# Five steps of a two-block transformer kernel put elsewhere in their engines' order, and one small transfer issued first

## The chip, the core and the metric

The kernel runs on one core of a Trainium2 chip. A core has a matrix engine (PE, TensorE), a vector engine (DVE, VectorE), an activation engine (ACT, ScalarE), a general engine (POOL, GpSimd) and a queue engine that only issues transfers (SP, SyncE). Each engine works through its own list of instructions in the order in which they are written; between engines there are only semaphores. The metric is the device time in microseconds (us), and less is better.

## The reference, cut to what matters

`x` is (16 sequences, 128 tokens, 128 channels) in float32, and `cond` is (16, 128). Two blocks follow each other.

```python
# block 0: one head of 128 channels, RMS norm, exact gelu
h = film(rmsnorm(x, norm1_w), cond, film1_w, film1_b)      # scale and shift for each sequence
x = x + (softmax(Q @ K.T * D**-0.5) @ V) @ proj_w + proj_b
h = film(rmsnorm(x, norm2_w), cond, film2_w, film2_b)
x = x + gelu(h @ mlp_w1 + mlp_b1) @ mlp_w2 + mlp_b2
# block 1: 16 heads of 8 channels, layer norm, padding mask, gates
mod = silu(cond) @ ada_w.T + ada_b                          # six rows for each sequence
h = modulate(layernorm(x), shift_msa, scale_msa)
x = x + gate_msa * attention(h, padding_mask)
h = modulate(layernorm(x), shift_mlp, scale_mlp)
x = x + gate_mlp * (gelu_tanh(h @ fc1_w.T + fc1_b) @ fc2_w.T + fc2_b)
```

## The kernel before

The whole of `x` stays in SBUF as `xs` (tokens on the partitions, 16 sequences). Tokens of one sequence are a tile of 128x128, and four sequences are a group, so that there are four groups `g` of `G = 4`. The order of the work is written out by hand, engine by engine; nothing schedules it. There are four stages, and the letter in front of a semaphore's name tells the stage.

Stage a is the attention of block 0, by groups. For a group, DVE takes statistics of `xs` (`statistics`, L844 to L854), POOL raises them to a power (`root`, L1115) and normalises (`norm`, L1134, into `xn`), PE turns the four tiles (`a_norm`, L239), ACT applies the film scale and shift (`affine`, L661, into `hT`), PE multiplies for Q and K (`a_qk`, L265) and for V (`a_value`, L270). DVE copies Q out of PSUM (`a_q`, L907), ACT copies K and V out (`a_kv`, L668 and L670). PE makes the scores (`a_scores`, L278), DVE their maxima (`a_max`, L913), ACT the exponentials (`a_exp`, L676), PE turns these (`a_turn`) and weights the values with them (`a_weighted`, L291), and DVE adds the result into `xs` (`a_residual`, L928). On PE the next group's products are interleaved: scores of group g, then Q, K and V of group g + 1, then turning and weighting of g. For group 0 alone, half of the normalising and of the film step is on DVE (L887, L892). After the first group's residual DVE also computes `silu` of the condition (L950, L952, L954), which PE needs only for the `ada` products behind the last group (L536).

Stage b is the MLP of block 0: `m_norm` (L239), `b_up` (four products of 128x512, L307, one for each quarter f of the hidden width), `b_gelus` on ACT (L703), `b_down` (L315), `b_residual` on DVE (L963).

Stage c is the attention of block 1, by sequences b = 0 to 15. Queries and keys are spread by transfers into padded tensors `q_pad`, `k_pad`, so that a head is 8 rows of a strip of 32. In a step b, PE does `first_slot(b)` (32 small products: half the scores of b and half the transposed scores of b - 2, L366), `between(b)` (four small steps of earlier or later sequences: `back_a`, `turn_maxima`, `back_b`, `turn_x` or `back_c`), `second_slot(b)` (the other halves), and `behind(b)` (`weighted(b - 3)`, L432, and one product of the next group's Q, K or V: `project`, L353, L356, L360). DVE takes the maxima (L1002), which each slot waits for because it writes the same PSUM banks again. ACT takes exponentials (L739), copies, and the modulation of a coming sequence (`front_h`, L718). POOL normalises coming sequences (`front_x`, L1189), prepares `x + gate * bias` (`prepare`, L1194, L1196) and adds the gated attention (`residual`, L1200, L1203). DVE takes the statistics of a finished sequence (`next_statistics`, L1019).

Stage d is the MLP of block 1. Its first normalisation, `d_norm(0)` and `d_norm(1)` (four instructions of L867 each), stands on DVE behind the steps 11 and 14 of stage c. PE turns the result in `m_norm("d_", 0, 6)`, behind step 12, and in `m_norm("d_", 1, 5)`, behind `weighted(B - 3, 4)` at the end of stage c. `d_bias` on POOL (L1214, L1217) prepares the last residual.

ACT's queue begins with three transfers: the film weights with the condition (L649), the bias rows (L650), the mask rows as integers (L651, 16 partitions of 128 numbers).

## Time and profile before

| what | value |
|---|---|
| median of 3 runs | 193.1 us (192.03 to 194.94) |
| the profiled execution's own time | 191.69 us |
| its span in the profile | 189.9 us |
| busy in that span | PE 173.1 us (91%), DVE 121.1 (64%), ACT 107.7 (57%), POOL 98.7 (52%) |
| stage a ends, about | 38.8 us |
| stage b's last up-product ends, about | 64 us |
| steps 2 to 15 of stage c | 77.2 to 148 us |

The span is what the profile covers, from the first instruction to the last; 1.8 us of the execution's time lie outside it. Busy shares are averages over four stages that differ, so the table tells which engine works most, and not where it waits.

### The profile page before, as it was taken

What the parts mean: (1) busy time and instruction counts of PE and PEld (TensorE: products, weight loads), DVE (VectorE), ACT (ScalarE), POOL (GpSimd) and SP (SyncE); (2) the same over time, 40 slices, a digit from 0 to 9 for tenths busy, and PEclk for the clock granted to TensorE, in tenths of its full rate; (3) what the DMA queues carried; (4) which work ended last, traced back from release to release, by engine and by line L of the source; (5) the groups of instructions that cost most, each with busy time, mean ns of one, the idle gap of its engine ahead of it and who ended that gap; (6) DMA issues with size and microseconds to landing.
All of it is one profiled execution on the core that took longest, in us unless ns stands there. A gap on an engine that the chain in (4) does not pass through costs nothing.

```text
span 189.9 us, 5687 instructions
## 1 busy us (share of the span) xinstructions
PE 173.1 (91%) x2250; PEld 134.2 (71%) x2250; DVE 121.1 (64%) x357; ACT 107.7 (57%) x272; POOL 98.7 (52%) x166
## 2 busy tenths in 40 slices
PE   6876989999699999889999999996997999999993
PEld 6744877587276698677678777875886765678592
DVE  0693598978005069768756876699489665596233
ACT  2336957862683751577577756673774785723500
POOL 5599949899900805994004333675145086691000
PEclk9999999999999999999999999998899999999999
DMA  5999999412650300300110000100000000001103
GB/s 126 345 430 423 433 412 431 177 43 52 217 224 0 114 0 3 116 5 5 57 60 3 7 35 31 57 5 2 5 7 7 2 3 0 5 0 55 59 0 110
DMA packets 5190, 19.31 MB, mean 102 GB/s; under 512 B 556, under 2 KB 1148, under 8 KB 3836
## 3 DMA queue, kind: packets, MB, share of 16 engines
q1 hardware_dynamic: 4844, 18.27, 25.0%
q10 hardware_dynamic: 320, 0.68, 1.2%
q8 instruction: 18, 0.29, 0.7%
q14 instruction: 8, 0.07, 0.1%
HBM read 7.24 MB, written 1.09 MB: 44 GB/s over the span
## 4 chain that ended last, share of the span: by engine, by line
PE 44%; issue 20%; POOL 19%; DVE 9%; DMA 3%; ACT 3%; POOLq 0%; DVEq 0%; ACTq 0%
PE ps L337 8%; PE ps L328 7%; PE ps L315 6%; PE ps L307 6%; POOL xb L1196 3%; POOL gtmp L1194 3%; POOL xc L1189 3%; PE ps L265 3%; POOL rstd L1115 3%; PE ps L366 2%; DMA xs<-x 2%; POOL xs L1203 2%; POOL gated L1200 2%; ACT hT L661 2%; DVE bn L844 2%
## 5 line engine op out<-in xcount | busy, mean ns | idle before, releaser
L1002 DVE TENSOR_REDUCE nm<-ps 128x4 f32<-128x512 f32 x64 | 42.0, 683 | 18.3 <-PE ps L366 17.9
L739 ACT ACTIVATE shared<-ps 128x512 f32<-128x512 f32 x64 | 34.5, 596 | 22.0 <-PE ps L366 21.9
L366 PE MATMUL ps<-k_pad,q_pad 32*128 32x128 f32 x512 | 35.4, 284 | 5.0 <-DVE nm L1002 4.7
L366 PEld LDWEIGHTS ps<-k_pad,q_pad 32*128 32x128 f32 x512 | 30.1, 188 | 13.2 <-issue 6.5
L366 PE MATMUL ps<-q_pad,k_pad 32*128 32x128 f32 x512 | 35.5, 285 | 0.1
L366 PEld LDWEIGHTS ps<-q_pad,k_pad 32*128 32x128 f32 x512 | 29.7, 188 | 0.5 <-DMA q_pad<-nmT 0.5
L1115 POOL TENSOR_TENSOR rstd<-var_eps,half 128x4 f32<-128x4 f32 x16 | 16.4, 1023 | 24.5 <-DVE var_eps L858 17.0
L1200 POOL TENSOR_TENSOR gated<-attn,gate 128x128 f32<-128x128 f32 x16 | 7.3, 459 | 40.8 <-ACT attn L758 40.7
L432 PE MATMUL ps<-shared,vx 128*32 128x128 f32 x512 | 17.9, 282 | 0.5 <-ACT attn L758 0.3
L785 ACT ACTIVATE hid<-ps,W 128x512 f32<-128x512 f32 x16 | 10.9, 689 | 9.7 <-PE ps L328 9.7
L307 PE MATMUL ps<-hT,W 128*128 128x512 f32 x32 | 14.6, 598 | 1.7 <-ACT hT L661 1.7
L661 ACT ACTIVATE hT<-ps,shift,scale 128x128 f32<-128x128 f32 x34 | 12.9, 467 | 5.2 <-PE ps L239 4.1
L432 PEld LDWEIGHTS ps<-shared,vx 128*32 128x32 f32 x512 | 13.6, 112 | 3.2 <-issue 1.7
L337 PEld LDWEIGHTS ps<-W,hid 128*128 128x128 f32 x128 | 14.7, 192 | 1.0 <-issue 1.0
L328 PE MATMUL ps<-hT,W 128*128 128x512 f32 x32 | 15.3, 599 | 0.0
L315 PE MATMUL ps<-W,hid 128*128 128x128 f32 x128 | 15.2, 276 | 0.0
L315 PEld LDWEIGHTS ps<-W,hid 128*128 128x128 f32 x128 | 14.8, 192 | 0.6 <-issue 0.5
L703 ACT ACTIVATE hid<-ps,W 128x512 f32<-128x512 f32 x16 | 10.7, 688 | 7.9 <-PE ps L307 7.8
L337 PE MATMUL ps<-W,hid 128*128 128x128 f32 x128 | 14.8, 275 | 0.0
L1189 POOL TENSOR_SCALAR xc<-xs,mean,rstd 128x128 f32<-128x128 f32 x16 | 12.6, 797 | 0.4
L844 DVE BATCH_NORM_STATS2 bn<-xs 128x6 f32<-128x128 f32 x44 | 9.5, 277 | 4.4 <-DMA xs<-x 4.2
L867 DVE TENSOR_SCALAR xn<-xs,stat,rstd 128x128 f32<-128x128 f32 x16 | 11.0, 749 | 1.7 <-POOL rstd L1115 1.7
(127 smaller groups left out, 321.9 us busy)
## 6 DMA issues: line engine op xcount, KB each, us to landing
q_pad<-hid SPq DMA_DIRECT2D x1, 4096.0 KB, 21.7
k_pad<-hid SPq DMA_DIRECT2D x1, 4096.0 KB, 30.6
gate<-gates SPq DMA_DIRECT2D x1, 2048.0 KB, 7.2
xs<-x SPq DMA_DIRECT2D x4, 256.0 KB, 6.4
gate<-mask SPq DMA_DIRECT2D x1, 1024.0 KB, 11.9
q_pad<-apT SPq DMA_DIRECT2D x4, 256.0 KB, 2.4
k_pad<-apT SPq DMA_DIRECT2D x4, 256.0 KB, 2.4
W<-weights SPq DMA_DIRECT2D x1, 768.0 KB, 9.9
```

What stands on the lines that cost most here:

```text
L307: mm(ps[:, f, :], w("mlp1", C, C * f), hT[g % 2][:], start=True, stop=True).then_inc(s["b_M1"], 1)
L315: ins = mm(bank(5)[:, j], hid[g % 2][:, f, j], w("mlp2", C, C * f), start=(f == 0), stop=(f == FC - 1), skip_group_check=True)
L328: mm(ps[:, UP_BANK[n], :], w("fc1", C, C * f), hT[g % 2][:], start=True, stop=True)\
L337: ins = mm(bank(o_bank)[:, j], hid[g % 2][:, f, j], w("fc2", C, C * f), start=(f == 0), stop=(f == FC - 1), skip_group_check=True)
L366: return mm(bank(to)[:, t], held[some, t, b], moved[some, t, b], start=True, stop=True, skip_group_check=True)
L432: ins = mm(ps[32 * j:32 * j + 32, to, N * e:N * e + N], v[:, e, j, s2], p[:, e, j, s2], start=(s2 == 0), stop=(s2 == 1), skip_group_check= ...
L661: ins = a(hT[g % 2][:, j], src[:, j], ACT.Identity, bias=shift[:, k, b:b + 1], scale=scale[:, k, b:b + 1])
L739: a(pT[b % 2][:, r], bank(of), ACT.Exp, scale=HD ** -0.5).then_inc(s["c_exp"], 1)
L844: v.bn_stats(bn[:, j], xs[:, G * g + j]).then_inc(ok, 1)
L1002: v.tensor_reduce(nm[b % 2][:, 4 * r:4 * r + 4], bank(of), AX.X, ALU.max, negate=True).then_inc(s["c_max"], 1)
L1115: p.tensor_tensor(rstd[:, k, G * g:G * g + G], var_eps[:, k, G * g:G * g + G], half[:, 0:G], ALU.pow)\
L1189: p.tensor_scalar(xc[b % 4][:], xs[:, b], mean[:, 0, b:b + 1], rstd[:, 2, b:b + 1], ALU.subtract, ALU.mult)\
```

## The change

Six edits, and no arithmetic is added or removed.

1. ACT's queue issues the mask rows first, the film weights second and the bias rows third.
2. In stage a, ACT copies K and V of group 0 ahead of the film step of group 1.
3. DVE computes `silu` ahead of its wait for the first turned tiles, and no longer behind the first residual.
4. In stage b, group 1: two of the four up-products, then the turning of group 2, then the other two; on ACT two gelus, the film step of group 2, two gelus.
5. The V product of the second group in stage c (four matmuls and their copy to `vx`, in bank 6) is cut in two halves of two matmuls, in bank 7, in the middle of the steps 2 and 3; the wait for it in `between(3)` goes, and `behind(b)` waits for it from b = 3 on.
6. `d_norm(0)` and `d_norm(1)` leave DVE; POOL does them as `first_norm` behind its `residual` of the steps 11 and 15, and `d_bias(0)` moves from step 11 to step 12.

```diff
--- before.py
+++ after.py
@@ -148,7 +148,7 @@
             ada_mm ada_ok gate_ok  wvp_mm wvp_ok bias_ok bcol_ok pbias_ok zero_ok pad_zero aug_ok aug_out aug_in maskb_ok c_vinit
             a_pow a_xn a_xb a_T a_h a_Q a_K a_V a_qT a_kT a_v a_S a_max a_exp a_PT a_pT a_PV a_rden a_res
             b_pow b_xn b_xb b_T b_h b_M1 b_gelu b_M2 b_res
-            c_pow c_xb c_gp c_xc c_Tx c_h c_Q c_K c_V c_q c_k c_v c_qs c_ks
+            c_pow c_xb c_gp c_xc c_Tx c_h c_Q c_K c_V c_q c_k c_v c_qs c_ks c_vh
             c_S c_max c_NT c_nm c_nms0 c_nms1 c_T c_exp c_PV c_oT c_T2 c_rden c_on c_T3 c_onT c_pr c_at c_ga c_res c_st
             d_var d_pow d_xn d_xb d_T d_h d_M1 d_gelu d_M2 d_gm d_gp d_res""".split()
         s = {n: sem(n) for n in names}
@@ -298,8 +298,8 @@
                     pe.wait_ge(s[p + "h"], g)
                 transposes(bank(t_bank), xn[g % 2], s[p + "T"])
 
-            def b_up(g):
-                for f in range(FC):
+            def b_up(g, fs=range(FC)):
+                for f in fs:
                     if f == 0:
                         pe.wait_ge(s["b_h"], g + 1)
                     if g:
@@ -361,6 +361,13 @@
                              skip_group_check=True)
                 ins.then_inc(s["c_V"], 1)
 
+            def second_value(half):
+                if half:
+                    pe.wait_ge(s["c_vh"], 1)
+                for j in (2 * half, 2 * half + 1):
+                    mm(ps[:, 7, N * (j % 2):N * (j % 2) + N], hc[1][:, j], w("v1"), start=True, stop=True,
+                       skip_group_check=True)
+
             def heads(held, moved, b, r, t, to):
                 some = slice(TILE * r, TILE * r + TILE)
                 return mm(bank(to)[:, t], held[some, t, b], moved[some, t, b], start=True, stop=True, skip_group_check=True)
@@ -454,7 +461,7 @@
             def between(b):
 
                 g = b - 1
-                if g % G < 3 and g // G + 1 < B // G:
+                if g % G < 3 and g != 2 and g // G + 1 < B // G:
                     pe.wait_ge(s[("c_q", "c_k", "c_v")[g % G]], g // G + 2)
                 if b == 13:
                     pe.wait_ge(s["d_h"], 1)
@@ -465,6 +472,8 @@
                     back_b(b - 5)
                 if b + LEAD < B:
                     pe.wait_ge(s["c_h"], b + LEAD)
+                    if b in (2, 3):
+                        second_value(b - 2)
                     turn_x(b + LEAD)
                 if b >= 6:
                     back_c(b - 6)
@@ -472,7 +481,7 @@
             def behind(b):
 
                 if b >= 3:
-                    pe.wait_ge(s["c_v"], (b - 3) // G + 1)
+                    pe.wait_ge(s["c_v"], max(2, (b - 3) // G + 1))
                     pe.wait_ge(s["c_h"], min(b + LEAD + 1, B))
                     if b >= 5:
                         pe.wait_ge(s["c_onT"], b - 4)
@@ -484,7 +493,7 @@
 
             def project(b):
                 g = b // G + 1
-                if g < B // G and b % G < 3:
+                if g < B // G and b % G < 3 and b != 2:
                     if b:
                         pe.wait_ge(s["c_nm"], b)
                     if b >= 4:
@@ -544,8 +553,9 @@
             mm(ps[:, 7, 3 * C:4 * C], bcol1[:], w("proj1"), start=False, stop=True, skip_group_check=True)\
                 .then_inc(s["ada_mm"], 1)
             b_down(0)
-            b_up(1)
+            b_up(1, range(2))
             m_norm("b_", 2, 4)
+            b_up(1, range(2, FC))
             b_up(2)
             m_norm("b_", 3, 4)
             pe.wait_ge(s["a_res"], B)
@@ -646,9 +656,9 @@
         @block.scalar
         def _(act):
             a = nc.scalar.activation
+            act.dma_start(mask_ri[:], mask).then_inc(s["mask_rin"], 16)
             act.dma_start(W[:, 0:W_AT["q"]], weights[:, 0:W_AT["q"]]).then_inc(s["w_film"], 16)
             act.dma_start(R[:, :], rows.partition_broadcast(128)).then_inc(s["rows_in"], 16)
-            act.dma_start(mask_ri[:], mask).then_inc(s["mask_rin"], 16)
 
             act.wait_ge(s["w_film"], 16)
             a(cond_e[:], w("cond", B), ACT.Exp, scale=-1.0).then_inc(s["silu_e"], 1)
@@ -683,8 +693,8 @@
             affine("a_", 0, 0, bank(0), range(2))
             act.wait_ge(s["wvp_mm"], 1)
             a(wvp[:], ps[:, 6, 0:C], ACT.Copy).then_inc(s["wvp_ok"], 1)
+            a_kv(0)
             affine("a_", 1, 0, bank(0))
-            a_kv(0)
             a_exp(0)
             for g in range(1, 4):
                 a_kv(g)
@@ -695,8 +705,8 @@
                 a_exp(g)
 
 
-            def b_gelus(g):
-                for f in range(FC):
+            def b_gelus(g, fs=range(FC)):
+                for f in fs:
                     act.wait_ge(s["b_M1"], FC * g + f + 1)
                     if g > 1:
                         act.wait_ge(s["b_M2"], g - 1)
@@ -705,8 +715,9 @@
             b_gelus(0)
             affine("b_", 1, 1, bank(4))
             act.wait_ge(s["pad_zero"], 32)
-            b_gelus(1)
+            b_gelus(1, range(2))
             affine("b_", 2, 1, bank(4))
+            b_gelus(1, range(2, FC))
             b_gelus(2)
             affine("b_", 3, 1, bank(4))
 
@@ -724,9 +735,16 @@
                     act.wait_ge(s["c_ks"], 16 * g)
                 a(k_sb[:], bank(K_BANK[g]), ACT.Identity, bias=col("cols1", COL1["k_b"])).then_inc(s["c_k"], 1)
 
+            def second_v(half):
+                v = ps[:, 7, 0:2 * N].rearrange("n (a k d) -> n a k d", k=2, d=HD)
+                slots = vx[1][:].rearrange("n b (a z) -> n (b a) z", z=64)[:, 16 * half:16 * half + 16]
+                for k in range(2):
+                    ins = a(slots[:, :, 48 * k:48 * k + HD], v[:, :, k], ACT.Copy)
+                ins.then_inc(s["c_v" if half else "c_vh"], 1)
+
             def front_v(g):
 
-                act.wait_ge(s["c_V"], g + 1)
+                act.wait_ge(s["c_V"], g + 1 if g < 2 else g)
                 v = ps[:, V_BANK[g], :].rearrange("n (a k d) -> n a k d", k=2, d=HD)
                 slots = vx[g % 2][:].rearrange("n b (a z) -> n (b a) z", z=64)
                 for k in range(2):
@@ -765,6 +783,8 @@
                     turned_o(b - 5)
                 if 0 < b and b + LEAD < B:
                     front_h(b + LEAD)
+                if b in (2, 3):
+                    second_v(b - 2)
                 if b >= 6:
                     projected(b - 6)
                 if b >= 2:
@@ -774,7 +794,7 @@
                     back_o(b - 3)
                 if b % G == 1 and b // G + 1 < B // G:
                     front_k(b // G + 1)
-                elif b % G == 2 and b // G + 1 < B // G:
+                elif b % G == 2 and b > 2 and b // G + 1 < B // G:
                     front_v(b // G + 1)
 
             def d_gelu(g, f):
@@ -886,6 +906,12 @@
             for j in range(2, G):
                 ins = v.tensor_scalar(xn[0][:, j], xs[:, j], rstd[:, 0, j:j + 1], None, ALU.mult)
             ins.then_inc(s["a_xd"], 1)
+            dve.wait_ge(s["silu_e"], 1)
+            v.tensor_scalar(cond_s[:], cond_e[:], 1.0, None, ALU.add).then_inc(s["silu_one"], 1)
+            dve.wait_ge(s["silu_one"], 1)
+            v.reciprocal(cond_r[:], cond_s[:]).then_inc(s["silu_one"], 1)
+            dve.wait_ge(s["silu_one"], 2)
+            v.tensor_tensor(silu[:], w("cond", B), cond_r[:], ALU.mult).then_inc(s["silu_ok"], 1)
             dve.wait_ge(s["a_T"], 1)
             dve.wait_ge(s["film_ok"], 2)
             for j in range(2, G):
@@ -944,14 +970,6 @@
                     a_max(g + 1)
                 a_residual(g)
                 dve.wait_ge(s["a_res"], G * (g + 1))
-                if g == 0:
-
-                    dve.wait_ge(s["silu_e"], 1)
-                    v.tensor_scalar(cond_s[:], cond_e[:], 1.0, None, ALU.add).then_inc(s["silu_one"], 1)
-                    dve.wait_ge(s["silu_one"], 1)
-                    v.reciprocal(cond_r[:], cond_s[:]).then_inc(s["silu_one"], 1)
-                    dve.wait_ge(s["silu_one"], 2)
-                    v.tensor_tensor(silu[:], w("cond", B), cond_r[:], ALU.mult).then_inc(s["silu_ok"], 1)
 
             statistics(1, 3)
 
@@ -1060,8 +1078,6 @@
             statistics(2, 3)
             for b in range(2, B):
                 step(b)
-                if b in (11, 14):
-                    d_norm((b - 11) // 3)
             turned_max(B - 1)
             normalise(B - 4)
             sums(B - 3)
@@ -1217,6 +1233,13 @@
                 p.tensor_tensor(xb[:, b:b + G], xs[:, b:b + G], gtmp[:], ALU.add).then_inc(s["d_xb"], 1)
                 pool.wait_ge(s["d_xb"], g + 1)
 
+            def first_norm(g):
+                pool.wait_ge(s["d_pow"], g + 1)
+                for j in range(G):
+                    b = G * g + j
+                    ins = p.tensor_scalar(xn[g][:, j], xs[:, b], stat[:, b, 0:1], rstd[:, 3, b:b + 1], ALU.subtract, ALU.mult)
+                ins.then_inc(s["d_xn"], 1)
+
             for b in range(B):
                 if b + LEAD + 1 < B:
                     if (b + LEAD + 1) % G == 0:
@@ -1228,8 +1251,12 @@
                 if b in (10, 14):
                     root(3, (b - 10) // G, s["d_pow"])
                 if b == 11:
+                    first_norm(0)
+                elif b == 12:
                     pool.wait_ge(s["c_xb"], b + 1)
                     d_bias(0)
+                elif b == 15:
+                    first_norm(1)
             pool.wait_ge(s["c_xb"], B)
             residual(B - 6)
             d_bias(1)
```

What stands on ACT at the start of stage a, before. L661 is the film step (first two tiles of group 0, then four tiles of group 1), L685 the copy of a weight product, L668 and L670 the copies of K and V, L676 the exponentials.

```order
L681 ACTIVATE gtmp,square_sum<-xs 128x128 x4
L661 ACTIVATE hT<-ps,shift,scale 128x128 x2
L685 ACTIVATE wvp<-ps 128x128
L661 ACTIVATE hT<-ps,shift,scale 128x128 x4
L668 ACTIVATE shared<-ps,W 128x512
L670 ACTIVATE shared<-ps 128x512
L676 ACTIVATE shared,aden<-ps,amax 128x128 x4
```

And after; the same instructions have the lines L691, L671, L695, L678, L680 and L686.

```order
L691 ACTIVATE gtmp,square_sum<-xs 128x128 x4
L671 ACTIVATE hT<-ps,shift,scale 128x128 x2
L695 ACTIVATE wvp<-ps 128x128
L678 ACTIVATE shared<-ps,W 128x512
L680 ACTIVATE shared<-ps 128x512
L671 ACTIVATE hT<-ps,shift,scale 128x128 x4
L686 ACTIVATE shared,aden<-ps,amax 128x128 x4
```

The two copies now stand ahead of the four film instructions of group 1.

On PE in stage b, the piece of the difference behind the `ada` products: L315 is `b_down(0)`, L307 the up-products of groups 1 and 2, L239 the turning of groups 2 and 3.

```order
 L315 MATMUL ps<-W,hid 128x128 x16
-L307 MATMUL ps<-hT,W 128x512 x4
-L239 MATMUL ps<-ident,xn 128x128 x4
-L307 MATMUL ps<-hT,W 128x512 x4
+L307 MATMUL ps<-hT,W 128x512 x2
+L239 MATMUL ps<-ident,xn 128x128 x4
+L307 MATMUL ps<-hT,W 128x512 x6
 L239 MATMUL ps<-ident,xn 128x128 x4
```

The turning of group 2 now stands behind the second up-product of group 1, not behind the fourth.

On POOL in the steps 11 to 13 of stage c, before: `prepare` (L1194, L1196), `residual` (L1200, L1203), and `d_bias(0)` (L1214, L1217).

```order
L1194 TENSOR_TENSOR gtmp<-gate,pbias 128x128
L1196 TENSOR_TENSOR xb<-xs,gtmp 128x128
L1200 TENSOR_TENSOR gated<-attn,gate 128x128
L1203 TENSOR_TENSOR xs<-gated,xb 128x128
L1214 TENSOR_TENSOR gtmp<-gate,R 128x512
L1217 TENSOR_TENSOR xb<-xs,gtmp 128x512
L1194 TENSOR_TENSOR gtmp<-gate,pbias 128x128
L1196 TENSOR_TENSOR xb<-xs,gtmp 128x128
L1200 TENSOR_TENSOR gated<-attn,gate 128x128
L1203 TENSOR_TENSOR xs<-gated,xb 128x128
```

And after, where L1240 is `first_norm(0)`; DVE's row of L867 behind its step 11 is gone.

```order
L1210 TENSOR_TENSOR gtmp<-gate,pbias 128x128
L1212 TENSOR_TENSOR xb<-xs,gtmp 128x128
L1216 TENSOR_TENSOR gated<-attn,gate 128x128
L1219 TENSOR_TENSOR xs<-gated,xb 128x128
L1240 TENSOR_SCALAR xn<-xs,stat,rstd 128x128 x4
L1210 TENSOR_TENSOR gtmp<-gate,pbias 128x128
L1212 TENSOR_TENSOR xb<-xs,gtmp 128x128
L1216 TENSOR_TENSOR gated<-attn,gate 128x128
L1219 TENSOR_TENSOR xs<-gated,xb 128x128
L1230 TENSOR_TENSOR gtmp<-gate,R 128x512
L1233 TENSOR_TENSOR xb<-xs,gtmp 128x512
```

Four instructions of the normalisation came in, and `d_bias(0)` went one step back.

## Rows read from the trace of the kernel before

**Rows 1.** The page: busy time, share of the span, instructions.

```profile
PE 173.1 (91%) x2250; PEld 134.2 (71%) x2250; DVE 121.1 (64%) x357; ACT 107.7 (57%) x272; POOL 98.7 (52%) x166
```

**Rows 2.** The chain that ended last, in order of time: start us, us, what.

```profile
143.51 1.52 DVE xn L867 x4
...
149.79 1.65 DMA q_pad<-nmT
```

**Rows 3.** Timeline from the start: start us, us, engine line, idle before.

```profile
5.13 0.87 DVE L844 BATCH_NORM_STATS2 bn<-xs 128x6 f32<-128x128 f32 x4 [4.25 <-DMA xs<-x]
...
9.47 0.73 DVE L892 TENSOR_SCALAR hT<-ps,scale,shift 128x128 f32<-128x128 f32 x2 [1.03 <-PE ps L253]
```

**Rows 4.** Timeline of PE and ACT, group 0 of stage a.

```profile
12.21 1.05 PE L270 MATMUL ps<-wvp,hT 128*128 128x128 f32 x8
13.74 1.51 ACT L661 ACTIVATE hT<-ps,shift,scale 128x128 f32<-128x128 f32 x4 [3.24 <-PE ps L239]
15.70 0.61 ACT L670 ACTIVATE shared<-ps 128x512 f32<-128x512 f32 x1
15.97 1.13 PE L278 MATMUL ps<-shared 128*128 128x128 f32 x8 [2.27 <-ACT shared L668]
16.94 1.88 PE L265 MATMUL ps<-hT,W 128*128 128x512 f32 x4
```

**Rows 5.** Timeline of POOL, DVE and PE, the rest of stage a.

```profile
21.87 3.54 POOL L1153 MEMSET vx<- 128x2048 f32 x2
22.42 1.88 PE L265 MATMUL ps<-hT,W 128*128 128x512 f32 x4
23.89 1.55 DVE L950 TENSOR_SCALAR cond_s<-cond_e 128x16 f32<-128x16 f32 x1
28.55 1.88 PE L265 MATMUL ps<-hT,W 128*128 128x512 f32 x4
33.88 3.67 PE L307 MATMUL ps<-hT,W 128*128 128x512 f32 x8
```

**Rows 6.** Timeline of POOL, PE and ACT, group 1 of stage b.

```profile
40.89 1.42 POOL L1134 TENSOR_SCALAR xn<-xs,rstd 128x128 f32<-128x128 f32 x4
45.10 3.60 PE L307 MATMUL ps<-hT,W 128*128 128x512 f32 x8
46.22 1.49 ACT L703 ACTIVATE hid<-ps,W 128x512 f32<-128x512 f32 x2 [5.01 <-PE ps L307]
50.88 3.70 PE L307 MATMUL ps<-hT,W 128*128 128x512 f32 x8 [1.74 <-ACT hT L661]
```

**Rows 7.** Timeline of PE and DVE, step 2 of stage c.

```profile
79.40 0.34 PE L366 MATMUL ps<-k_pad,q_pad 32*128 32x128 f32 x1 [0.68 <-DVE nm L1002]
80.51 1.16 PE L360 MATMUL ps<-W,hc 128*128 128x128 f32 x8
80.62 1.29 DVE L1002 TENSOR_REDUCE nm<-ps 128x4 f32<-128x512 f32 x2 [0.69 <-PE ps L366]
```

**Rows 8.** Timeline of POOL, DVE, PE and ACT, steps 11 to 13 of stage c.

```profile
125.07 0.46 POOL L1203 TENSOR_TENSOR xs<-gated,xb 128x128 f32<-128x128 f32 x1
126.61 2.64 DVE L867 TENSOR_SCALAR xn<-xs,stat,rstd 128x128 f32<-128x128 f32 x4
129.91 0.37 PE L366 MATMUL ps<-k_pad,q_pad 32*128 32x128 f32 x1 [1.99 <-DVE nm L1002]
133.84 1.51 ACT L661 ACTIVATE hT<-ps,shift,scale 128x128 f32<-128x128 f32 x4 [0.59 <-PE ps L239]
```

**Rows 9.** A window of 2 us in step 12: its columns stand below.

```profile
132.00:134.00 2.00, 2.00 (x24) 1.28 (x20) 0.81 (x3) 0.87 (x4) 0.00 (x0) 0.50 0.04 8
```

**Rows 10.** Groups by line on POOL: busy us, mean ns, idle before.

```profile
L1189 POOL TENSOR_SCALAR xc<-xs,mean,rstd 128x128 f32<-128x128 f32 x16 | 12.6, 797 | 0.4
```

**Rows 11.** Timeline of PE and POOL, the end of stage c.

```profile
145.69 0.37 PE L366 MATMUL ps<-k_pad,q_pad 32*128 32x128 f32 x1 [1.26 <-DVE nm L1002]
...
151.57 0.46 POOL L1200 TENSOR_TENSOR gated<-attn,gate 128x128 f32<-128x128 f32 x1 [5.37 <-ACT attn L758]
```

The columns of the row of group 9 are: the window, its length, then for PE, PEld, DVE, ACT and POOL the busy time with the number of instructions, then the granted clock of TensorE as a share of its full speed, the busy share of the transfer engines and GB/s.

## The prediction

> **What bounds the kernel now.** I read the page first. PE is busy for 173.1 of 189.9 us [rows 1], so a gain must come from PE's 17 us of idle time, from matmuls that run at a lower clock, or from waits that the page counts as busy because an engine holds a stalled instruction. Next came the chain of waits. It runs on PE nearly everywhere in stages a, b and d, and leaves it at a few places, two of which are touched here: `d_norm(1)` on DVE, and at the end of stage c the transfer of the turned maxima [rows 2]. Then I went along the timeline of PE, noting each idle time of over 0.5 us and what ended it. The large ones are 2.27 us before the first scores, 1.74 us in stage b, 1.99 us and 1.26 us in stage c [rows 4, 6, 8, 11]. Every one of the four is addressed by an edit. PE runs its list in order, so what it saves at one place moves everything behind it, as long as no transfer or other engine with a time of its own becomes last. The working below is therefore a sum of shifts of PE's list.
>
> **Edit 1, the first transfers.** The statistics of the first group start when `x` lands, at 5.13 [rows 3]; the film weights land at about the same time, and are now issued about 0.45 us later. DVE has 1.03 us of idle time before L892 [rows 3] in which lateness is hidden, and `x` has the transfer engines to itself a little longer, so it can land earlier. I take 0, with bounds of 0.3 us gained and 0.5 us lost.
>
> **Edit 2, K and V of group 0 first.** ACT now waits idle for 3.24 us, until the tiles of group 1 are turned at 13.70, and spends 1.51 us on them before it copies K [rows 4]; PE waits for that copy until 15.97. The V product ends at 13.26 [rows 4], and K's stands before it, complete by about 12.4. So K is copied from 12.4 to 13.1 (15.25 to 15.97 is 0.7 us now), V from 13.3 to 13.9 (0.61 us), and the scores start at 13.75, right behind the turning. The film step of group 1 starts at 13.9, 0.16 us later than now, ends at 15.4, and the next Q and K products start at 15.47 where they started at 16.94 [rows 4]: 1.47 us gained. The 2.27 us don't all come back, because PE next waits for the film step.
>
> **Edit 3, `silu`.** It takes DVE from 23.89 to 25.94. L950 alone lasts 1.55 us for 16 numbers in each partition, and it ends with POOL's memset at 25.41 [rows 5]. Its new place is DVE's idle 1.03 us [rows 3]; without the stall I estimate the three instructions at 0.7 us, so they are hidden there unless edit 1 takes that room too (then up to 0.4 us). Without them, Q of group 2 is copied as soon as it is there, and PE needs 5.5 us from one group's Q to the next (16.94 to 22.42) and not 6.1 (22.42 to 28.55) [rows 4, 5]. The products of group 3 start at 15.47 + 5.49 + 5.49 = 26.45 and not 28.55: 2.1 us. On the way to `b_up(0)` DVE is last again: statistics of 1.5 us, the maxima of group 2 at 27.6, exponentials to 29.1, K and V copied to 30.35, the film step to 31.9. `b_up(0)` starts at 31.97 and not 33.88 [rows 5]. **Edits 2 and 3 give 1.9 us.** From below they give 0.6 (the difference of the two intervals alone), from above 2.27 + 2.05 = 4.3; I take the worked value.
>
> The row of L950 leaves two readings. If 1.55 us were its own time, `silu` would last 2.0 us in its new place, 1.0 us more than DVE's idle time, the first film step would be that much later, and edits 2 and 3 would give 0.9 us. The end beside the memset's speaks for the other reading. In words of the Trainium skill, page "SBUF — State Buffer", section "Who interferes with whom", DVE in a two-port mode and POOL take one port pair as an exclusive lock, and whoever comes second waits for the other's whole instruction; by this rule the time is the memset's, and the sum stays at 1.9 us.
>
> **Edit 4, stage b.** PE is idle for 1.74 us before `b_up(2)` [rows 6]: the film step of group 2 waits for the turning, which stands behind all four up-products of group 1 though its tiles were normalised by 42.3 [rows 6]. Now two products end at 46.85 in old times, the turning at 47.4, and the two others at 49.0. ACT's first two gelus end at 47.71 [rows 6], its film step at 49.25, and its other two gelus at 50.6. `b_up(2)` starts at 49.33 and not 50.88. Its third product needs the third gelu, done at 49.95, and starts at 51.05. **1.55 us gained**, with bounds of 0.8 (if a gelu comes in PE's way) and 1.74. The normalised tiles of stage c are also needed earlier, at 53.3; POOL has them at 52.05 since it hangs on `b_residual(0)` alone. The zeros and mask rows of the padded tensors come by transfers with times of their own; their transfer was issued by 40, the scores need it at about 61.6.
>
> **Edit 5, the second V product.** The four matmuls of step 2 go (1.16 us with overlap, 1.08 to the next slot), but they hid a wait. The slot behind them needs DVE's maximum, which starts at 80.62 and lasts 0.65 [rows 7], so it could start at 81.5 where it starts at 81.59. The halves, of about 0.45 us each, fall where PE is idle, 0.68 us in step 2 and 0.52 in step 3, waiting for DVE [rows 7]. In step 3 the copy of the second half must be done before `weighted(0)`: ACT ends it at 84.6 and PE wants it at 84.6. **I take 0**, bounds 0.15 gained and 0.4 lost.
>
> **Edit 6, the normalisations of stage d.** `d_norm(0)` holds DVE for 2.64 us, the maximum that PE's second slot of step 12 needs stands behind it, and PE waits 1.99 us [rows 8]. That is not all. In the window 132 to 134 the granted clock is 0.50 [rows 9], the lower of TensorE's two levels (1.2 instead of 2.4 GHz), after PE had been idle from 127.92 to 129.91. From that slot to ACT's film step 3.93 us pass (129.91 to 133.84 [rows 8]), though a slot (1.1), `weighted` (1.0) and the turning (0.6) take 2.7 us at full clock. Without stall and low clock: second slot 127.95, turning done at 130.6, film step of 1.51 us from 130.7 to 132.2. PE waits for it some 0.6 us (its next slot ends at 131.6), and `between(13)` starts at 132.25 and not at 135.40: **3.15 us**, bounds 1.96 (the clock falls all the same) and 3.8 (ACT not in the way).
>
> POOL needs 0.79 us for each such instruction [rows 10], 3.15 for a group. It is free at 125.53 [rows 8], so the group is done at 128.7, before PE wants it at 130.0. `residual(6)` ends at 130.6 and not 130.1, in time for DVE's statistics behind the maxima of step 12. `d_bias(0)` then ends at 133.15 and `residual(7)` at 135.1, while DVE comes to its statistics at 135.5. `d_norm(1)` stands on the chain with 1.52 us [rows 2] and makes PE wait 1.26 us [rows 11]. Without it the slot starts right behind `between`: **1.25 us**, bounds 0 and 1.26. On POOL it starts at 143.05 in the new time (its `residual(9)` comes with ACT) and ends at 146.2. PE would turn it at 150.72 - 4.4 = 146.3, and behind that waits for the transfer of the maxima (1.65 us [rows 2]) until 147.05 anyway. POOL's idle 5.37 us [rows 11] takes up the rest.
>
> The page "GPSIMD Engine Reference", section "Engine selection", of the Trainium skill speaks against this edit: elementwise work belongs on VectorE, since GpSimd is about twice as slow for two inputs. The rows do show twice the time for this form, 0.79 us against the 0.38 of `d_norm(1)`. By the page the edit would lose 1.6 us a group if POOL were the bound. That is a rival below.
>
> **The sum.** 0 + 1.9 + 1.55 + 0 + 3.15 + 1.25 = 7.85 us. The profiled execution took 191.69 us with a span of 189.9, so it becomes 183.8 with a span of 182.1. The median of the three runs is 1.4 us above that execution; I keep this difference and predict **185.2 us**.
>
> **The rivals.**
> - *Stage a doesn't pay.* POOL is busy there from 9 to 25.8 with hardly a gap, and `norm(1, 0)` hangs on it. If POOL, or `silu` in its new place, becomes last, edits 1 to 3 give nothing: 193.1 - 5.95 = 187.1. Against it speaks that POOL's tiles for group 3 are done at 19.5 and PE wants them at 23.6. Chance 0.10. If only the film weights come too late, by 1 us past the idle time: 186.2, chance 0.03.
> - *The low clock comes somewhere else.* It cost about 1.2 us in step 12 (3.93 against 2.7). PE was idle for 2.27 us in stage a [rows 4] and the clock stayed up, so idle time alone doesn't settle it, and it may come at another gap. Then 186.4; chance 0.08.
> - *POOL becomes the bound in steps 12 to 15*, as the page on GpSimd would have it: `residual` comes late, DVE's statistics hold the next maxima, and edit 6 gives about 1 us instead of 4.4. 193.1 - 4.45 = 188.6; it decides from a lateness of 0.5 us in step 13. Chance 0.07.
> - *Slower than before.* The four POOL instructions take much longer beside DVE's work, as L867 did beside POOL's (2.64 instead of 1.52 us). In PE's list the turning stands in front of all of step 13. From 2.4 us for one instruction the lateness (7 us for each group) eats more than the sum. At 3 us each, both groups come 7.5 us late: 193.1 - 3.45 + 15 = 204.6. POOL's own row shows at most 0.80 us. Chance 0.02.
>
> **How the numbers follow.** The forecast (gain 6 to 9.5 us) has 0.70. The range should leave out 2 in 10: with all bounds at their worst the sum is 2.5 us (190.6), which needs several misses at once, and at their best over 11 us. I take 182.8 to 189.6. A change of 2% (3.9 us, to 189.2) is about what a measurement of this kernel can tell from none. Faster by more than that are the forecast and the first three rivals but for a part: 0.90; within 2%: 0.08; slower: 0.02.
>
> **What would show it.** In the new profile: scores of group 0 at about 13.8, the product of `b_up(0)` at about 32.0, no idle time over 0.4 us between the two parts of stage b's products, no idle time of PE over 1 us in the steps 12 and 15, granted clock 1.00 all through them, `first_norm` rows of about 0.79 us, and a wait of some 0.6 us of PE for ACT's film step in step 13. Wrong would be a new idle time before L366 that DVE's statistics end, POOL on the chain in the steps 12 to 15, or a first group that starts later than now.

## The result and the profile after

The changed kernel takes **184.16 us** in the median of 4 executions (183.2 to 186.04), against 193.1 us before. The ratio is 0.9538, with a 95% interval of 0.9466 to 0.9611. In a second set of runs it took 184.09 us (183.2 to 186.26, 6 executions) against 192.17, a ratio of 0.9566 [0.9513, 0.9618]. The forecast was 185.2 us. The profiled execution took 184.48 us with a span of 182.7 us; the sum had put these at 183.8 and 182.1. Here and in all that follows, executions over 1.5% slower than the fastest of the same kernel count as slow, and ratios and spans compare the others.

The page of the kernel after, busy time by engine, to be read beside [rows 1]:

```profile
PE 172.7 (95%) x2250; PEld 134.4 (74%) x2250; DVE 116.2 (64%) x349; ACT 107.5 (59%) x274; POOL 104.9 (57%) x174
```

PE works as long as before; its share rose because the span shrank by 7.2 us. POOL has 8 instructions more and DVE 8 fewer: edit 6.

**The start** is the part that did not go as forecast. First two rows of PE's timeline in the kernel before, the film products and the first Q product:

```profile
5.49 0.96 PE L498 MATMUL ps<-W 128*128 128x16 f32 x8
...
10.39 1.98 PE L265 MATMUL ps<-hT,W 128*128 128x512 f32 x4 [0.52 <-ACT hT L661]
```

Now the kernel after: the chain of waits, then the timeline of ACT and PE (start us, us, engine line, idle time before), then three windows in the columns of [rows 9]:

```profile
0.72 0.41 ACTq L659
...
1.17 5.42 DMA W<-weights
...
7.70 2.45 PE ps L245 x12
...
11.96 1.98 PE ps L265 x4
```

```profile
6.61 0.22 ACT L664 ACTIVATE cond_e<-W 128x16 f32<-128x16 f32 x1 [3.21 <-DMA W<-weights]
6.63 1.06 PE L507 MATMUL ps<-W 128*128 128x16 f32 x8 [1.21 <-DMA W<-weights]
11.96 1.98 PE L265 MATMUL ps<-hT,W 128*128 128x512 f32 x4 [0.31 <-ACT hT L671]
```

```profile
6.00:8.00 2.00, 1.37 (x11) 1.37 (x12) 0.56 (x4) 1.39 (x9) 1.47 (x3) 0.97 1.03 394
8.00:10.00 2.00, 2.00 (x12) 2.00 (x11) 1.68 (x10) 0.00 (x0) 1.83 (x4) 0.50 1.01 319
10.00:12.00 2.00, 1.69 (x10) 1.50 (x8) 0.96 (x4) 0.90 (x3) 1.51 (x5) 0.67 1.05 431
```

The film weights are issued 0.45 us later (1.17 instead of 0.72) and land 1.28 us later (ACT reads them at 6.61; before, at 5.33). PE is idle for 1.21 us, and in the windows behind it the granted clock is at the lower of its two levels: twelve warming matmuls (L245) take 2.45 us of the chain. The first Q product starts at 11.96 and not at 10.39.

**Stages a and b**, timeline of PE after, to be read beside [rows 4 to 6]:

```profile
15.11 1.06 PE L278 MATMUL ps<-shared 128*128 128x128 f32 x8
16.97 1.10 PE L265 MATMUL ps<-hT,W 128*128 128x512 f32 x2 [0.80 <-issue]
...
33.44 3.67 PE L307 MATMUL ps<-hT,W 128*128 128x512 f32 x8
...
44.66 1.88 PE L307 MATMUL ps<-hT,W 128*128 128x512 f32 x4
46.38 0.60 PE L239 MATMUL ps<-ident,xn 128*128 128x128 f32 x4
```

The idle time of 2.27 us before the scores of group 0 is gone. `b_up(0)` starts at 33.44 and not at 33.88, although the first Q product is 1.57 us late: from the one to the other 21.48 us pass instead of 23.49. The turning now stands between two halves of `b_up(1)`, and the idle time of 1.74 us before `b_up(2)` is gone too; the chain of waits has `b_up(2)` at 48.71, where it was at 50.88:

```profile
48.71 3.70 PE ps L307 x8
```

**Stage c**, timelines of PE and POOL after, beside [rows 7, 8, 11]:

```profile
77.24 0.34 PE L373 MATMUL ps<-k_pad,q_pad 32*128 32x128 f32 x1 [0.24 <-DVE nm L1020]
79.25 0.34 PE L373 MATMUL ps<-k_pad,q_pad 32*128 32x128 f32 x1 [0.83 <-DVE nm L1020]
...
129.72 0.44 PE L448 MATMUL ps<-ident,oT 128*128 128x128 f32 x2 [0.49 <-ACT hT L671]
```

```profile
122.93 3.13 POOL L1240 TENSOR_SCALAR xn<-xs,stat,rstd 128x128 f32<-128x128 f32 x4
...
140.51 3.15 POOL L1240 TENSOR_SCALAR xn<-xs,stat,rstd 128x128 f32<-128x128 f32 x4
144.67 0.46 POOL L1216 TENSOR_TENSOR gated<-attn,gate 128x128 f32<-128x128 f32 x1 [1.01 <-ACT attn L776]
```

No idle time is left before the second slots of steps 12 and 15 (they had 1.99 and 1.26 us), and the granted clock stays at 1.00 through both. POOL takes 3.13 and 3.15 us for a group, 0.78 us for an instruction. PE waits 0.49 us for ACT's film step in step 13. After the second group POOL is still idle for 1.01 us: it never became the bound.

### The profile page after: what moved, and what is told of

Read it like the earlier page. It is cut to its first block, busy times and chain, and to the rows that moved or that the text cites. A ratio compares the mean times of both kernels' runs of the same rounds, so it can differ in the third digit from the quotient of the medians.

```text
span 182.7 us, 5687 instructions
## 1 busy us (share of the span) xinstructions
PE 172.7 (95%) x2250; PEld 134.4 (74%) x2250; DVE 116.2 (64%) x349; ACT 107.5 (59%) x274; POOL 104.9 (57%) x174
## 4 chain that ended last, share of the span: by engine, by line
PE 86%; DVE 5%; DMA 4%; issue 2%; ACT 1%; ACTq 0%
PE ps L373 19%; PE ps L439 8%; PE ps L315 8%; PE ps L337 8%; PE ps L328 8%; PE ps L307 6%; PE ps L265 4%; DMA W<-weights 3%; PE ps L239 3%; PE ps L448 3%; PE ps L353 2%; PE ps L356 2%; PE ps L270 2%; PE ps L459 2%; PE ps L291 2%
## 5 line engine op out<-in xcount | busy, mean ns | idle before, releaser
L373 PE MATMUL ps<-q_pad,k_pad 32*128 32x128 f32 x512 | 35.0, 283 | 0.1
L439 PE MATMUL ps<-shared,vx 128*32 128x128 f32 x512 | 17.3, 275 | 0.3
L439 PEld LDWEIGHTS ps<-shared,vx 128*32 128x32 f32 x512 | 13.1, 109 | 3.0 <-issue 1.5
L328 PE MATMUL ps<-hT,W 128*128 128x512 f32 x32 | 15.3, 599 | 0.0
L315 PE MATMUL ps<-W,hid 128*128 128x128 f32 x128 | 15.2, 276 | 0.0
L315 PEld LDWEIGHTS ps<-W,hid 128*128 128x128 f32 x128 | 14.8, 192 | 0.6 <-issue 0.5
L671 ACT ACTIVATE hT<-ps,shift,scale 128x128 f32<-128x128 f32 x34 | 12.8, 463 | 3.4 <-PE ps L253 3.1
L307 PE MATMUL ps<-hT,W 128*128 128x512 f32 x32 | 14.7, 598 | 0.0
L729 ACT ACTIVATE hc<-ps,shift,scale 128x128 f32<-128x128 f32 x16 | 6.8, 469 | 7.6 <-PE ps L349 7.6
```

The source lines that it names most:

```text
L307: mm(ps[:, f, :], w("mlp1", C, C * f), hT[g % 2][:], start=True, stop=True).then_inc(s["b_M1"], 1)
L315: ins = mm(bank(5)[:, j], hid[g % 2][:, f, j], w("mlp2", C, C * f), start=(f == 0), stop=(f == FC - 1), skip_group_check=True)
L328: mm(ps[:, UP_BANK[n], :], w("fc1", C, C * f), hT[g % 2][:], start=True, stop=True)\
L373: return mm(bank(to)[:, t], held[some, t, b], moved[some, t, b], start=True, stop=True, skip_group_check=True)
L439: ins = mm(ps[32 * j:32 * j + 32, to, N * e:N * e + N], v[:, e, j, s2], p[:, e, j, s2], start=(s2 == 0), stop=(s2 == 1), skip_group_check= ...
L671: ins = a(hT[g % 2][:, j], src[:, j], ACT.Identity, bias=shift[:, k, b:b + 1], scale=scale[:, k, b:b + 1])
```

## The experiments

Two quantities are used below. One is the place of a certain instruction in the profiled execution. The other is each execution's own span with its own mean granted clock. The mean clocks stand in three heaps: 0.997 to 1.0 (no fall of the clock), 0.988 to 0.991 (one fall, as in the profile of the kernel before, whose windows show one stretch at the lower level, in step 12 [rows 9]) and 0.974 to 0.982 (two, as in the profile of silu_only below). The kernel before was executed 58 times beside these experiments: one execution has no fall, 31 have one and 26 have two. **A fall costs about 1.2 us** (1.2 and 1.3 by the medians in the table, 1.1 and 1.3 in traces below), and kernels are best compared at the same number of falls. For the kernel before, "no fall" is a single execution, so the comparisons at no fall rest on it.

| kernel | no fall | one | two |
|---|---|---|---|
| before | 188.8 (1) | 190.0 (30) | 191.3 (19) |
| changed kernel, both sets | 181.5 (5) | 182.6 (2) | |
| it without edit 1 (film_first) | 181.2 (6) | | |
| mask_only | 188.65 (2) | 190.3 (3) | 191.2 (1) |
| kv_only | 189.0 (6) | 190.15 (4) | |
| silu_only | | 189.9 (5) | 191.2 (6) |
| kv_silu | 186.6 (1) | 188.45 (4) | |
| split_only | 187.2 (3) | 188.3 (4) | 189.9 (3) |
| v_only | 188.05 (2) | 189.4 (3) | 190.2 (1) |
| norm0_only | 187.0 (2) | 187.9 (4) | |
| norms_only | 185.5 (4) | 186.85 (2) | |

Median span in us, with the number of executions. Where the text counts how many executions have a fall, it counts all of them.

### film_first: the change without edit 1

```
-            act.dma_start(mask_ri[:], mask)
             act.dma_start(W[:, 0:W_AT["q"]], weights[:, 0:W_AT["q"]])
             act.dma_start(R[:, :], rows.partition_broadcast(128))
+            act.dma_start(mask_ri[:], mask)
```

> The changed kernel with edit 1 alone undone: ACT issues film weights, bias rows, mask rows. Theory (the late film weights cost what the first group lost): the first turned tiles of stage a come at 8.8 us as in the kernel before, not at 9.9, the first Q product at 10.4 and not at 11.96, and everything behind is 1.6 us earlier, span about 181.1. Rival (DVE's idle time hid the lateness, and the start was late for another reason, such as silu in its new place): first Q product at 11 us or later, span within 0.4 us of 182.7.

Measured: 183.02 us (182.79 to 184.73), ratio 0.9531 [0.948, 0.9582], span of the profiled execution 181.0. Timelines of ACT and PE and a window:

```profile
5.23 0.22 ACT L664 ACTIVATE cond_e<-W 128x16 f32<-128x16 f32 x1 [1.83 <-DMA W<-weights]
...
10.30 1.97 PE L265 MATMUL ps<-hT,W 128*128 128x512 f32 x4 [0.53 <-ACT hT L671]
```

```profile
8.00:10.00 2.00, 1.71 (x14) 1.27 (x12) 1.93 (x9) 0.70 (x4) 1.83 (x5) 1.00 1.04 383
```

The weights land where they did before, PE has no gap (its film products start at 5.94, behind the warming matmuls), the clock stays at 1.00, and the first Q product starts at 10.30. **Edit 1 costs 1.7 us in the profiled execution (182.7 against 181.0) and 0.3 us in the median span where the clock doesn't fall (181.5 against 181.2).** The intervals of the ratios overlap (this one with 0.9538 [0.9466, 0.9611] and 0.9566 [0.9513, 0.9618] of the changed kernel), so the loss is read from the traces and not from the times. Edits 2 to 6 alone are worth 8.9 us of span in the profiled executions (189.9 against 181.0), which includes the one fall that the kernel before has there. Two of the six executions have spans of 182.7 and 182.9 without a fall, where the others have 181.0 to 181.2; what they did is open.

### mask_only: the kernel before with edit 1 alone

```
+            act.dma_start(mask_ri[:], mask)
             act.dma_start(W[:, 0:W_AT["q"]], weights[:, 0:W_AT["q"]])
             act.dma_start(R[:, :], rows.partition_broadcast(128))
-            act.dma_start(mask_ri[:], mask)
```

> The kernel before with edit 1 alone. Theory: the film weights land at 6.6 us and not at 5.3, the clock of TensorE is at its lower level from about 8 to 11 us, the first Q product starts 1.6 us late, span about 191.4. Rival (only with silu in its new place is the start late): span within 0.4 us of 189.9.

Measured: 193.18 us (190.39 to 195.42), ratio 0.996 [0.9909, 1.0011], span 190.6: only 0.7 us longer than before, less than expected, although the first Q product starts 2.4 us late, at 12.78. Timeline of PE, DVE and PE again, and two windows:

```profile
7.25 0.96 PE L498 MATMUL ps<-W 128*128 128x16 f32 x6 [1.87 <-DMA W<-weights]
26.28 0.37 DVE L950 TENSOR_SCALAR cond_s<-cond_e 128x16 f32<-128x16 f32 x1
131.72 0.37 PE L366 MATMUL ps<-k_pad,q_pad 32*128 32x128 f32 x1 [1.99 <-DVE nm L1002]
```

```profile
8.00:10.00 2.00, 2.00 (x11) 2.00 (x11) 1.28 (x8) 0.62 (x5) 1.82 (x4) 0.50 1.01 354
...
132.00:134.00 2.00, 2.00 (x66) 1.68 (x62) 1.97 (x5) 1.02 (x3) 0.78 (x2) 1.00 0.01 4
```

The loss is given back in two places. L950 of `silu` takes 0.37 us and not 1.55 [rows 5], because it comes late enough to meet only the end of POOL's memset; `b_up(0)` is at 35.70, 1.82 us late and no longer 2.39. And in step 12 the same idle time of 1.99 us before L366 is *not* followed by the low clock, so PE gains 1.1 us from there to step 13. Which gap is followed by a fall differs from execution to execution; at equal falls edit 1 costs the old kernel nothing at none (188.65 against 188.8) and 0.3 us at one (190.3 against 190.0). Neither expectation was met: the span lies between the two.

### more_warm: fourteen warming matmuls instead of ten

```
-            warm(10)
+            warm(14)
```

> The changed kernel with 14 instead of 10 warming matmuls ahead of the film products, so that PE is hardly idle while it waits for the film weights. Theory of two parts: of the 1.57 us about 1.0 is the lower clock behind PE's idle 1.2 us, 0.5 the lateness itself; then the first Q product starts at about 11.0 and the span is about 181.7. Rival (the lateness is all): first Q product at 11.9, span 182.7. If the four matmuls outlast the landing, they add up to 0.5 us.

Measured: 183.81 us (183.59 to 184.05), ratio 0.9544 [0.9499, 0.9589], span 182.3. ACT's row:

```profile
6.92 0.22 ACT L664 ACTIVATE cond_e<-W 128x16 f32<-128x16 f32 x1 [3.51 <-DMA W<-weights]
```

This lies between the two expectations. The clock is at 1.00 all through, as the theory said, and the first Q product starts at 11.57; but the extra matmuls outlasted the landing, and the film products began at 7.64, 0.7 us after it. The filler takes away the fall and most of the scatter (0.46 us from lowest to highest), not the lateness.

### late_film: the film weights a little later, with nothing ahead of them

```
-            act.dma_start(mask_ri[:], mask)
+            act.wait_ge(s["ident_ok"], 1)
             act.dma_start(W[:, 0:W_AT["q"]], weights[:, 0:W_AT["q"]])
             act.dma_start(R[:, :], rows.partition_broadcast(128))
+            act.dma_start(mask_ri[:], mask)
```

> The changed kernel with the old order of ACT's three transfers, but ACT waits for POOL's first memset ahead of the first, so the film weights are issued some 0.3 us later than in the kernel before with no transfer ahead of them. If it is the time of the issue that counts, they land at 6.0 to 6.6 us and the first Q product starts between 10.9 and 12.0. If it is the mask transfer ahead of them, they land at about 5.6 and the first Q product starts before 10.8.

Measured: **182.52 us** (182.38 to 182.84), ratio 0.9483 [0.9442, 0.9524], span 181.0. Timelines of ACT's queue, of ACT and of PE:

```profile
0.95 0.40 ACTq L660 DMA_DIRECT2D W<-weights  x1
...
5.54 0.21 ACT L665 ACTIVATE cond_e<-W 128x16 f32<-128x16 f32 x1 [1.75 <-DMA W<-weights]
...
10.27 1.98 PE L265 MATMUL ps<-hT,W 128*128 128x512 f32 x4 [0.52 <-ACT hT L672]
```

The first Q product starts where it does in film_first, as expected if the transfer ahead is what counts. The weights are read at 5.54, which is hardly later than in the nine traces with the issue at 0.72 (5.23 to 5.53), and PE's warming matmuls hide even that: the film products start at 5.94 here and in film_first. So half of edit 1's delay of 0.45 us costs nothing. With the 8 KB of mask rows ahead, ACT read the weights at 6.61, 6.92, 7.21 and 7.23 in four traces; with nothing ahead at 5.23 to 5.54 in ten. The two groups don't touch: 0.22 us more of delay and one small transfer ahead are worth at least 1.07 us. This version has the lowest median of all that ran, 1.6 us below the changed kernel and 0.5 us below film_first, and little scatter (0.46 us from the lowest to the highest, 1.94 in film_first); the intervals of the three ratios overlap, though.

### after_again: the changed kernel once more

> The changed kernel once more, to see how often its start runs at the lower clock. The runs so far list a span and a mean granted clock each: 182.7 us at 0.989 in the profiled one, 182.1 and 181.4 at 1.0. Theory: the late film weights cost 0.3 us where the clock stays up and 1.3 us more where it falls at the start, so the spans fall into two groups, near 181.4 with a mean clock of 1.0 and near 182.7 with 0.99. Rival: the 1.6 us of the first Q product are the wait itself, and the spans lie in one group near 182.5 whatever the clock.

Measured: 184.09 us, spans 181.4, 181.5, 182.1, 184.3 and 184.5 at a mean clock of 0.997 to 1.0, and 182.5 at 0.989. Timeline of PE:

```profile
7.23 1.06 PE L507 MATMUL ps<-W 128*128 128x16 f32 x8 [1.08 <-DMA W<-weights]
8.15 1.58 PE L245 MATMUL ps<-ident 128*128 128x128 f32 x12
...
11.27 1.96 PE L265 MATMUL ps<-hT,W 128*128 128x512 f32 x4 [0.54 <-ACT hT L671]
```

Here the wait of 1.08 us isn't followed by a fall, the twelve warming matmuls take 1.58 us, and the first Q product starts at 11.27. The two traces of this one kernel part what the wait costs from what the fall costs. From the film products to the first Q product 4.04 us pass here (7.23 to 11.27) and 5.33 in the first trace (6.63 to 11.96): **the fall is 1.3 us of the start.** The rest is lateness: beside film_first, whose film products start at 5.94, they are 1.29 us late here and the Q product 0.97; in the first trace they were 0.69 us late, which leaves 0.4 of its 1.66 us once the fall is taken off. Of the ten executions of the two sets, three lie near the theory's 181.4 with no fall and two near 182.7 with one; two lie at 182.1 with no fall, among them this one, whose weights landed later than in the first trace (read at 7.21 and not 6.61), so the lateness itself costs 0.3 to 1.0 us, not always 0.3. Three (184.2 to 184.5) lie above both, with no fall recorded; what they did is open. The rival, one heap near 182.5 whatever the clock, fits less: the two executions with a fall are the two whose mean clock is 0.989.

### kv_only: edit 2 alone

```
-            affine("a_", 1, 0, bank(0))
             a_kv(0)
+            affine("a_", 1, 0, bank(0))
             a_exp(0)
```

> The kernel before with edit 2 alone (K and V of group 0 copied ahead of the film step of group 1). Theory: the scores of group 0 start at 13.75 instead of 15.97 and the third group's first product at about 21.0 instead of 22.42, but it brings little by itself, because silu still stands on VectorE's list until POOL's memset ends (25.41): the fourth group's products stay within 0.3 us of 28.55 and b_up(0) within 0.4 us of 33.88; span 189.6 to 189.9 where the clock falls once. Rival: the gain of 1.5 us of the first interval is kept to the end, span 188.4.

Measured: 191.44 us (190.62 to 193.77), ratio 0.995 [0.9913, 0.9987], spans 189.0 without a fall and 190.15 with one, where the kernel before has 188.8 and 190.0. Edit 2 alone brings nothing at equal clock. The ratio is below 1 because falls are rarer: six of twelve executions have none, against one of 58 of the kernel before. Timeline of POOL, DVE and PE:

```profile
22.46 3.55 POOL L1153 MEMSET vx<- 128x2048 f32 x2
24.17 1.87 DVE L950 TENSOR_SCALAR cond_s<-cond_e 128x16 f32<-128x16 f32 x1
27.25 1.16 PE L278 MATMUL ps<-shared 128*128 128x128 f32 x8 [0.91 <-DVE shared L907]
```

DVE comes earlier to `silu` relative to the memset, stalls for 1.87 us instead of 1.55, ends 0.03 us after it again (26.04 and 26.01), and PE waits for DVE. The scores of group 0 can't be compared directly, since this execution's first Q product is at 12.13; from there to the scores 3.15 us pass (5.58 before). From the first Q product to `b_up(0)` 22.34 us pass and not 23.49; how much of that is the edit can't be told, because a late start alone shortens the stretch (22.92 in mask_only, which has the old order here).

### silu_only: edit 3 alone

```
             ins.then_inc(s["a_xd"], 1)
+            dve.wait_ge(s["silu_e"], 1)
+            v.tensor_scalar(cond_s[:], cond_e[:], 1.0, None, ALU.add).then_inc(s["silu_one"], 1)
...
+            v.tensor_tensor(silu[:], w("cond", B), cond_r[:], ALU.mult).then_inc(s["silu_ok"], 1)
             dve.wait_ge(s["a_T"], 1)
```

and the same instructions taken out behind `a_residual(0)`.

> The kernel before with edit 3 alone (silu moved to VectorE's idle time ahead of the first Q statistics). Theory: the scores of group 0 stay at 15.97 and the third group at 22.42, the fourth group's products come at 27.9 instead of 28.55 and b_up(0) at about 33.25 instead of 33.88; span 189.2. Rival: all of the 2.05 us that silu held VectorE come back, b_up(0) at 31.9, span 187.9.

Measured: 192.86 us (191.27 to 195.3), ratio 1.0015 [0.998, 1.005]. Spans 189.9 with one fall and 191.2 with two: 0.1 us below the kernel before at as many falls, though 0.7 was expected. Timeline of PE, then two windows:

```profile
16.21 1.64 PE L278 MATMUL ps<-shared 128*128 128x128 f32 x8 [2.27 <-ACT shared L668]
17.63 3.10 PE L265 MATMUL ps<-hT,W 128*128 128x512 f32 x4
```

```profile
18.00:20.00 2.00, 2.00 (x3) 0.67 (x2) 0.98 (x2) 1.40 (x8) 1.90 (x6) 0.50 1.01 430
...
134.00:136.00 2.00, 2.00 (x24) 1.67 (x24) 0.18 (x1) 1.31 (x5) 0.00 (x0) 0.50 0.03 8
```

In this execution the clock fell behind the gap of 2.27 us in stage a, where it had stayed up in the profiled execution of the kernel before, and again in step 12. The four Q products take 3.10 us instead of 1.88. The interval from the third group to the fourth is 5.44 us (6.13 before), so the 0.69 us are there; but split_only, which has `silu` in its old place and a late third group too, shows 5.44 as well. A delay of the third group hides the stall by itself. The two traces are a fair pair, since both have a fall behind the gap in stage a: from the first Q product to `b_up(0)` 24.62 us pass here and 24.61 in split_only, so edit 3 alone gave nothing there. What it would give in a stage a without a fall is seen in no trace; the spans allow 0.1 us.

### kv_silu: edits 2 and 3

The two diffs above together.

> The kernel before with edits 2 and 3. Theory: the two are worth more together than the sum of each alone (0.2 and 0.6 us), as the prediction had it: scores of group 0 at 13.75, fourth group's products at about 26.4, b_up(0) at about 31.9, 1.9 to 2.0 us gained, span 187.9 to 188.0 where the clock falls once. Rival: they add, and the span is 189.1.

Measured: 190.24 us (188.42 to 191.86), ratio 0.9887 [0.9832, 0.9942]; spans 186.6 without a fall, 188.5 with one. Timeline of DVE and PE:

```profile
8.72 0.27 DVE L890 TENSOR_SCALAR cond_s<-cond_e 128x16 f32<-128x16 f32 x1
...
13.40 1.06 PE L278 MATMUL ps<-shared 128*128 128x128 f32 x8
...
31.73 1.53 PE L307 MATMUL ps<-hT,W 128*128 128x512 f32 x3
```

From the first Q product to `b_up(0)` 21.46 us pass instead of 23.49: **2.03 us, of which edit 2 alone brings nothing to the end and edit 3 alone almost nothing.** At equal clock the spans say 1.55 and 2.2 us, the latter from one execution each. The two are worth more together than apart. L950 alone lasts 0.27 us here.

### split_only: edit 4 alone

```
-            b_up(1)
+            b_up(1, range(2))
             m_norm("b_", 2, 4)
+            b_up(1, range(2, FC))
             b_up(2)
```

with the gelus on ACT split in the same way.

> The kernel before with edit 4 alone (b_up of group 1 split around the turning of group 2). Theory: b_up(0) stays at 33.88, PE's idle time of 1.74 us before b_up(2) goes, and b_up(2) starts at 49.2 instead of 50.88 as in the changed kernel, where the same distance shrank by 1.73 us; the gain is kept to the end, span 188.2 where the clock falls once. Rival: something behind it is late (the zeros and mask rows of the padded tensors), and the span is over 189.

Measured: 190.37 us (189.0 to 191.88), ratio 0.9874 [0.9832, 0.9915]; spans 187.2, 188.3 and 189.9, which is 1.6, 1.7 and 1.4 us below the kernel before at as many falls. The profiled execution had two falls (span 190.0). Timeline of PE:

```profile
46.51 1.88 PE L307 MATMUL ps<-hT,W 128*128 128x512 f32 x4
48.23 0.60 PE L239 MATMUL ps<-ident,xn 128*128 128x128 f32 x4
48.67 5.60 PE L307 MATMUL ps<-hT,W 128*128 128x512 f32 x12
```

The twelve products behind the turning (the rest of group 1 and all of group 2) run without a gap. From `b_up(1)` to the first scores of stage c 18.29 us pass instead of 20.01: 1.72 us, all kept. The rival, a late transfer behind it, is out.

### v_only: edit 5 alone

```
+                if b in (2, 3):
+                    second_value(b - 2)
-                if g < B // G and b % G < 3:
+                if g < B // G and b % G < 3 and b != 2:
```

`second_value` issues two of the four products; ACT copies each half.

> The kernel before with edit 5 alone (second V product in two halves in steps 2 and 3). Theory: 0.27 us, as the distance from step 2 to step 4 shrank in the changed kernel: idle time before the second slot of step 2 down from 0.68 to 0.25 us, about 0.8 us before the next slot, which waits for VectorE's maxima; span 189.6 where the clock falls once. Rival, the prediction's value: 0, span 189.9.

Measured: 191.19 us in the median, ratio 0.992 [0.9879, 0.9961]; spans 188.05, 189.4 and 190.2 at none, one and two falls, 0.6 to 1.1 us below the kernel before, and more than the 0.27 expected. The profiled execution took 345.52 us, so it isn't read for this question. The prediction's 0 is out. How much of the gain is in the steps 2 to 4 is seen in the changed kernel alone, below.

### norm0_only: only the first normalisation of stage d on POOL

```
-                if b in (11, 14):
-                    d_norm((b - 11) // 3)
+                if b == 14:
+                    d_norm(1)
```

and `first_norm(0)` on POOL, as in the change.

> The kernel before with only the first group's normalisation of stage d on POOL; the second one stays on VectorE behind step 14. Theory: the idle time of 1.99 us in step 12 goes and with it the reason for the low clock there, so between(13) starts at about 132.3 instead of 135.40, 3.1 us gained, of which 1.3 us are the clock; every run shows a mean clock of 0.998 or more, span 186.8. Rival: only the idle time comes back and the clock falls all the same, mean clock 0.99, span 187.9 to 188.1.

Measured: 189.66 us (188.65 to 189.75), ratio 0.984 [0.9806, 0.9873]. Timeline of PE:

```profile
132.38 0.44 PE L441 MATMUL ps<-ident,oT 128*128 128x128 f32 x2 [0.49 <-ACT hT L661]
...
142.68 0.37 PE L366 MATMUL ps<-k_pad,q_pad 32*128 32x128 f32 x1 [1.27 <-DVE nm L1002]
```

From the first slot of step 12 to that of step 13 4.70 us pass instead of 7.79: 3.09 us, and the windows from 130 to 136 stand at 1.00. At equal falls the spans are 1.8 and 2.1 us below the kernel before, so about 2 us are the idle time and the rest is the fall that no longer comes. But four of six executions still show one fall (0.988 to 0.99), against the expectation that none would; a second place where the clock can fall, the gap of 2.27 us in stage a, is untouched in this kernel. In which gap those four fell isn't recorded.

### norms_only: edit 6 alone

> The kernel before with edit 6 alone (both first normalisations of stage d on POOL). Theory: 3.1 us at the first and 1.25 us at the second, idle time before the second slot of step 15 gone, span 185.5, mean clock 1.0. Rival: the second is hidden behind the transfer of the turned maxima, and the span equals that of the kernel with the first one alone.

Its diff is that of norm0_only with `first_norm(1)` on POOL too. Measured: 187.36 us (187.26 to 188.69), ratio 0.9758 [0.9717, 0.98], span 185.6. Timeline of POOL:

```profile
143.18 3.12 POOL L1222 TENSOR_SCALAR xn<-xs,stat,rstd 128x128 f32<-128x128 f32 x4
147.34 0.45 POOL L1198 TENSOR_TENSOR gated<-attn,gate 128x128 f32<-128x128 f32 x1 [1.04 <-ACT attn L758]
```

The second slot of step 15 starts 10.72 us after the first one of step 13, where 11.97 us passed in norm0_only: 1.25 us for the second normalisation. The rival, that the transfer of the maxima hides it, is out. The mean clock of 1.0 that was expected came in four of six executions; two have a fall. Edit 6 is the largest part of the change.

## Why the prediction was right, and where not

The forecast was 185.2 us, and 184.16 was measured. The mechanism was right for edits 2, 3, 4 and 6, which are nearly all of the gain. Three sizes were wrong, and that they left only 1.0 us between them is luck: edit 1 cost 1.7 us in the profiled execution, the other edits gave 1.05 us more than the sum had, and the correction behind the sum was 1.7 us too high.

**Edit 1: forecast 0, measured a loss of 0.3 to 1.7 us. This is the step that failed.** The prediction assumed that a transfer issued 0.45 us later lands about that much later, with 0.5 us lost as the worst case and DVE's 1.03 us of idle time as a cover. The cover was there: in after_again the film products start 1.74 us later than in the kernel before (7.23 and 5.49) and the first Q product 0.88 us later (11.27 and 10.39), so 0.86 us are hidden. What was wrong is the landing, 1.28 us later in the profiled execution and 1.6 to 1.9 in the others, and what the sum left out is that the matmul engine's wait can be followed by a fall of the clock, 1.3 us. The mask rows did land sooner, and `x` did too (DVE's first statistics start at 4.79 instead of 5.13), but nobody was waiting for either. "A first group that starts later than now", named as a sign that something is wrong, came true. The rival with the film weights 1 us past the idle time had this mechanism with a chance of 0.03: far too little, for a price that rested on an assumed landing.

**Edits 2 and 3: forecast 1.9, measured 2.01 (changed kernel) and 2.03 (kv_silu).** The reading of L950's row was right. Its length follows the memset's end: 1.55, 1.87 and 0.37 us in the old place (before, kv_only, mask_only), ending 0.03 us behind the memset each time; 0.20 us in split_only, where it starts after the memset has ended; and 0.16 to 0.27 us in the new place. That is what the Trainium skill, page "SBUF — State Buffer", section "Who interferes with whom", says of the shared port pair, and the traces agree. The three instructions took 0.66 us, estimated at 0.7. What the prediction had not worked out is that each alone is worth almost nothing.

**Edit 4: forecast 1.55, measured 1.73 (changed kernel), 1.72 (split_only).** `b_up(2)` starts 0.18 us earlier than worked out. The wait of its third product for the third gelu did not come either: the eight products take 3.70 us, as before [rows 6].

**Edit 5: forecast 0 with at most 0.15 gained, measured 0.42 in the traces, 0.6 to 1.1 in spans.** From the first scores of stage c to step 4, 0.20 us are gained: the wait before the second slot of step 2 falls from 0.68 to 0.24 us, and 0.83 us come in front of the next slot. Another 0.22 us come in step 8, where PE no longer waits 0.32 us for ACT's `attn` copy. That this too is edit 5's doing was not tested apart; the wait is in every trace without edit 5 and in none of the readable ones with it. What the spans show beyond 0.42 is open.

**Edit 6: forecast 3.15 + 1.25, measured 3.09 + 1.25 (norm0_only, norms_only) and 3.09 + 1.24 (changed kernel).** The wait for ACT's film step was forecast at 0.6 and is 0.49. The rivals with POOL fall: its instructions take 0.78 us. The Trainium skill, page "GPSIMD Engine Reference", section "Engine selection", has GpSimd about twice as slow for elementwise work on two inputs and calls work on one input "roughly line-rate". The prediction laid the factor of two beside this row, but the instruction has one tensor input, with two scalars for each partition, and takes 0.78 us on POOL against 0.38 on DVE. So what the Trainium skill says of one input does not hold for this form. The price did not matter, since POOL had the time.

**The low clock.** The prediction gave 1.2 us of edit 6 to it. At equal falls edit 6 is worth 3.15 to 3.3 us, and in step 12 the fall itself costs 1.12 us: from the second slot to step 13 5.49 us pass in the kernel before and 4.37 in mask_only, with the same wait in front. So that was sized well. But it treated the fall in step 12 as a fixed part of the kernel before. The runs show three gaps after which the clock may fall: the one at the start that edit 1 opens (1.08 to 1.87 us), the one before the scores of group 0 (2.27), and the one in step 12 (1.99). With all three closed (film_first, late_film) or filled (more_warm) none of 18 executions has a fall. With the first alone open (the changed kernel) 2 of 10 have one; with the second alone open of these three (norms_only) 2 of 6; with the third alone (kv_silu) 5 of 6; with the last two open (before) 57 of 58 have one or two. "The low clock comes somewhere else" therefore did happen, in a fifth of the executions, and at the start. The list of places may not be complete: in kv_only, whose gap in stage a is closed, two of twelve executions have two falls, and no trace shows where the second is.

**From the sum to the median.** The prediction added 1.4 us, the distance of the old kernel's profiled execution from its median. That distance looks like executions with a second fall, which the change removes: the new median lies 0.3 us below the profiled execution. The clocks behind the median of 193.1 aren't on record, but of the 58 executions of the kernel before those with a time of 193.0 or more all have two falls but one. This error of 1.7 us upward outweighed the error in the sum, which was 0.7 us too optimistic (183.8 against 184.48). Summed up, edits 2 to 6 gave 8.9 us of span where 7.85 were forecast (8.5 in the parts above, 0.1 at the first Q product, 0.3 behind stage c), and edit 1 took 1.7.

## What to carry to other kernels

In this kernel the transfer that the first real products wait for belongs first on its queue, and a change there is judged by the landing, not by the issue: 0.45 us of issue, with a small transfer ahead, were 1.3 to 1.9 us of landing here. A gap of the matmul engine is also a place where its clock can fall, and one fall (about 1.2 us) is not much less than edit 4 is worth (1.7 us), so kernels are compared at equal mean clock. And two waits that cover each other are removed together: an edit that brings nothing alone may be worth 2 us beside another.

## What the runs showed of the hardware that was not expected

- The landing time jumps. The same 272 KB, issued at 0.72 or 0.95, are read at 5.23 to 5.54 (ten traces); issued at 1.17 behind an 8 KB transfer on the same queue, at 6.61 to 7.23 (four traces). Whether the small transfer or the last 0.22 us of delay does it was not tried apart.
- A gap doesn't decide whether the clock falls: the idle time of 1.99 us in step 12 is followed by 0.50 in the kernel before and by 1.00 in mask_only, kv_only and kv_silu; that of 2.27 us in stage a by the lower level in silu_only and split_only and by 1.00 in the kernel before and norm0_only.
- Matmuls can run at little over half their pace with a recorded clock of 1.00. Timelines of PE in kv_only and in film_first, the same twelve warming matmuls, both in windows with a granted clock of 1.00 (at the lower level they took 2.45 us of the chain in the changed kernel):

```profile
7.50 2.91 PE L245 MATMUL ps<-ident 128*128 128x128 f32 x12
```

```profile
6.98 1.58 PE L245 MATMUL ps<-ident 128*128 128x128 f32 x12
```

kv_only's first Q product starts 1.7 us later than that of the kernel before. In v_only's profiled execution such a pace lasted to the end: L328's matmuls take 1149 ns in the mean (599 in the changed kernel), the page shows a clock of 1.00 and 343.7 us of span. A mean clock of 1.00 is no proof of full speed; the duration of a known matmul is.
